# Graph attention and expert layers on one core: packets of one row for x and x1, and a longer lead for the gathers

## What is computed

```
def gnn(x):                                    # x is normalised row by row before this
    xt = matmul(x, weight).reshape(N, 4, 64)
    alpha = softmax(leaky_relu(einsum(xt[src], attn_l) + einsum(xt[dst], attn_r), 0.01), axis=1)
    tmp = einsum('nh,nhd->nd', alpha[:N], xt[dst[:N]])
    return broadcast(tmp, heads)               # the same 64 numbers for each head
x1  = x + gnn(layernorm(x))
z   = layernorm(x1)
out = x1 + z + sum over the 2 best of 8 experts e of  share_e * (gelu(z @ w1[e] + b1[e]) @ w2[e] + b2[e])
```

## Time and profile before

| | us |
|---|---|
| three runs: median (lowest to highest) | 481.96 (478.07 to 485.9) |
| the profiled execution: its own time | 482.41 |
| the profiled execution: span from the first to the last instruction | 480.7 |
| TensorE busy in the span | 385.5 |
| VectorE busy | 345.6 |
| ScalarE busy | 276.4 |
| GpSimd busy | 242.7 |

### The profile page before, as it was taken

How to read it: one execution, slowest core, us unless ns; L and a number is a source line. 1 busy time by engine, 2 the same in 40 slices (tenths; PEclk the granted TensorE clock), 3 DMA queues, 4 the chain that set the end, 5 groups by cost and what they waited for, 6 DMA issues and landing times.

```text
span 480.7 us, 11417 instructions
## 1 busy us (share of the span) xinstructions
PE 385.5 (80%) x3546; PEld 336.0 (70%) x3546; DVE 345.6 (72%) x1158; ACT 276.4 (58%) x715; POOL 242.7 (50%) x241
## 2 busy tenths in 40 slices
PE   3587999796999783545598989989999999999750
PEld 2476888685888673534487978878888788888740
DVE  1628859796979697969277868787788788778530
ACT  3138645363636364574176676777777777867530
POOL 7557867585848530000644544555644565554422
PEclk9597979596969796555599999999999999999885
DMA  4254725656565643021322322222222222221110
GB/s 149 76 150 135 198 78 152 194 154 197 152 191 140 203 121 124 14 92 55 81 62 75 82 64 65 68 80 81 74 65 68 84 88 68 81 69 58 58 44 20
DMA packets 18334, 48.23 MB, mean 100 GB/s; under 512 B 4719, under 2 KB 9354, under 8 KB 18276
## 3 DMA queue, kind: packets, MB, share of 16 engines
q0 software_dynamic: 10896, 29.61, 21.2%
q1 hardware_dynamic: 6626, 17.32, 12.1%
q10 hardware_dynamic: 756, 0.58, 0.4%
HBM read 34.42 MB, written 13.07 MB: 99 GB/s over the span
## 4 chain that ended last, share of the span: by engine, by line
PE 60%; DVE 13%; ACT 10%; issue 7%; DMA 4%; another core or an unknown queue 4%; POOL 1%; DVEq 0%; ACTq 0%; POOLq 0%
PE bank L1442 17%; PE bank L1425 16%; PE bank L1260 7%; PE bank L1389 4%; PE bank L1251 3%; PE bank L1284 3%; PE bank L1436 3%; PE bank L1263 3%; PE bank L1274 2%; DMA out_dram<-acc,order 2%; DMA work<-token_table,order 1%; PE bank L1375 1%; DVE row_out L986 1%; DVE work L955 1%
## 5 line engine op out<-in xcount | busy, mean ns | idle before, releaser
L475 POOL DMA_INDIRECT acc<-in_x_dram,index x98 | 112.5, 1148 | 53.7 <-ACT work L563 24.5
L512 POOL DMA_INDIRECT work<-token_table,order x76 | 74.8, 985 | 101.1 <-DVE order L1136 57.1
L693 ACT ACTIVATE h<-bank,b_col 128x128 f32<-128x128 f32 x250 | 78.0, 365 | 56.9 <-PE bank L1425 49.1
L1425 PE MATMUL bank<-work,w_hi 128*128 128x128 f16 x1000 | 100.0, 222 | 2.5 <-DVE work L1170 2.2
L1425 PE MATMUL bank<-work,w_lo 128*128 128x128 f16 x500 | 92.5, 222 | 0.0
L1425 PEld LDWEIGHTS bank<-work,w_hi 128*128 (+1 forms) x1000 | 83.2, 100 | 7.0 <-DVE work L1170 3.0
L521 POOL DMA_INDIRECT out_dram<-acc,order x49 | 49.5, 1011 | 75.7 <-DVE acc L1204 29.2
L1204 DVE SCALAR_TENSOR_TENSOR acc<-bank,work,acc 128x256 f32<-128x256 f32 (+1 forms) x125 | 60.4, 483 | 27.1 <-PE bank L1442 23.6
L1260 PE MATMUL bank<-w_ext,work 128*128 128x260 f32 x196 | 63.4, 454 | 16.3 <-ACT work L556 13.9
L1186 DVE SCALAR_TENSOR_TENSOR h_lo<-h,h_hi 128x256 f16<-128x256 f32 x125 | 52.6, 421 | 24.6 <-ACT h_hi L699 16.4
L1442 PE MATMUL bank<-w_hi,h_lo 128*128 (+1 forms) x250 | 69.2, 277 | 0.0
(11 more groups left out here) (208 smaller groups left out, 719.0 us busy)
## 6 DMA issues: line engine op xcount, KB each, us to landing
token_table<-row_out SPq DMA_DIRECT2D x7, 931.0 KB, 5.2
acc<-in_x_dram SPq DMA_DIRECT2D x7, 784.0 KB
work<-in_L_ffn_w_dram SPq DMA_DIRECT2D x16, 256.0 KB
acc<-in_x_dram,index POOLq DMA_INDIRECT x98
work<-token_table,order POOLq DMA_INDIRECT x76
out_dram<-acc,order POOLq DMA_INDIRECT x49
acc<-in_x_dram SPq DMA_DIRECT2D x7, 105.0 KB
w_raw<-in_L_gnn_weight_dram ACTq DMA_DIRECT2D x1, 256.0 KB
```

The source lines that it names most:

```text
L475: nc.gpsimd.indirect_dma_start(out=xds[:, t % RING, n, :], out_offset=None, in_=x, in_offset=bass.IndirectOffsetOnAxis(ap=index[:, n, t:t ...
L512: nc.gpsimd.indirect_dma_start(out=rows[:, k % ROWS_RING, :], out_offset=None, in_=table, in_offset=bass.IndirectOffsetOnAxis(ap=order[:, ...
L693: last = nc.scalar.activation(h32[:, i % RINGS, f * P:(f + 1) * P], bank[i % RINGS][:, f * P:(f + 1) * P], ACT.Gelu, bias=bias_of(f), scal ...
L1425: last = nc.tensor.matmul(bank[i % RINGS][:, f * P:(f + 1) * P], first_weights(i, lo, c, f), x2T[:, r, half, c * P:(c + 1) * P], start=(m ...
```

## The change

The padding of 16 numbers (APART) behind every row of `xres` and of `row_out` in SBUF keeps a partition's seven rows apart. The operations on them, the bytes moved and the layout in HBM stay. `x1T` moves up by 224 numbers a partition within `acc`. PACE goes from 5 to 8: tile t is gathered once tiles 0 to t - 9 are projected, and the wait begins with tile 9 instead of tile 6.

```
-PACE = 5
+PACE = 8
...
+APART = 16
...
-        xres = flat_acc[:, cut:cut + 2 * GT * D].rearrange("p (b t d) -> p b t d", b=2, t=GT)
-        cut += 2 * GT * D
+        xres = flat_acc[:, cut:cut + 2 * GT * (D + APART)].rearrange("p (b t d) -> p b t d", b=2, t=GT)[:, :, :, 0:D]
+        cut += 2 * GT * (D + APART)
         x1T = flat_acc[:, cut:cut + GT * D].rearrange("p (t k c) -> p t k c", t=GT, k=KT)
...
-        row_out = sb("row_out", [P, 2, GT, ROW])
+        row_apart = sb("row_out", [P, 2, GT, ROW + APART])
+        row_out = row_apart[:, :, :, 0:ROW]
```

## The result

| | before | after |
|---|---|---|
| median of 4 runs, side by side | 480.87 us (478.07 to 485.9) | 488.02 us (485.31 to 489.43) |
| profiled execution: span | 480.7 us | 487.1 us |

The ratio is 1.0218, with a 95% interval from 1.0173 to 1.0263. The prediction was 477.5 us.

What follows compares the result with a forecast made beforehand. No engine was full: each group loops through several, VectorE nearest its limit at some 84%. Terms 482.4 + 0 + 0 + 0 - 4.4 gave 478.0 us for a profiled execution, 477.5 for a median; range 467 to 488.

Steps and rivals of the forecast that it cites:

- (a): SP's loads of x: 1,024-byte packets instead of 7,168 are no slower, 2.6 to 3.2 us either way; term 0.
- (b): SP's x1 stores in 1,064-byte packets: last store delays expert pieces once, -1.0 to +2.1 us, taken as 0; 10.9 to 25.8 GB/s.
- The stall: ScalarE's wait for the last expert pieces, line 551: growth from 4.75 to 7 us would show slow small writes.
- (c): GpSimd's gathers start up to three tiles earlier; nobody waited for them, so direct gain 0.
- well under 17.6: Sign of being right: GpSimd's wait for ScalarE's copy at line 563 falls well under 17.6 us.
- (d): ScalarE's four "remote" idle stretches at group ends (4.23 to 7.10 us) shrink if long packets cause them; -4.4 us, a third of -13.1.
- the larger share for queue 0: Sign of being right: in windows with both queues loaded, queue 0 (the gathers) gets a larger share.
- The share of 0.8: Gathers' share beside x if DMA engines switch queues per packet: 0.8 with 1,024 against 4,096 bytes, 0.36 with 7,168.
- nothing happens: Rival: stretches belong to TensorE's completions under full DMA engines, however bytes are cut; 482 us, chance 0.30 (480 to 484).
- The slower one: Rival: extra gathers fall into store and expert pieces, 1.8 us more in each of four groups; 489 us, chance 0.12.
- Full relief: Rival: all four stretches go, with VectorE's 13.1 us; groups of 21.3 us, 468.9 us in all, chance 0.18.
- The four groups that I had counted: Seven-tile groups between 74.7 and 172.9 us, where VectorE's waits from the stretches total 13.1 us, the full-relief gain.

Runs made afterwards that it cites:

- eight at the start: Against the kernel before: lead of eight for the gathers of tiles 6 to 13 alone, five from tile 14, packets as before; 480.62 us, 1.0108.
- eight afterwards: Against the kernel before: lead of five for tiles 0 to 13, eight from tile 14 on, packets as before; 486.01 us, 1.0267.
- the run with eight and pauses: Against the kernel before: lead of eight, and at every third tile GpSimd waits until the gather of the tile before has landed; 508.67 us, 1.0507.
- the run with twelve gathers: Against the kernel before: lead of three for the first ten tiles, twelve extra gathers into unread memory behind tile 3's gather; 494.48 us, one execution.
- the last sitting: Fifth sitting: kernel before 456.82 us; x's padding alone, lead five, 455.3 us (0.9993); lead three for ten tiles plus delayed second x, 456.17 us (1.004).
- the run with narrow gathers: Lead of eight, gathers bringing 64 of each row's 256 numbers, the rest set to 1.0 by a VectorE memset; 495.72 us, one execution.

## Why the prediction was wrong

**(a) Packets of x, 0: right.** x was read at 0.84 MB in 4 us with a share of 0.770, 17.0 GB/s for one busy engine, against 17.9 in large pieces. SP's queue from 112 to 116 us in the kernel after:

```profile
q1 hardware_dynamic: 855, 0.84, 77.0%
```

**(b) Packets of x1, taken as 0, within -1.0 to +2.1: mis-sized.** The stall grew by 1.5 us (6.29 against 4.75), in the run with the padding alone by 2.2. The last store, at 192.9 to 197 us, alone on the queues:

```profile
q1 hardware_dynamic: 804, 0.86, 93.0%
```

That is 14.1 GB/s for one engine, nearer to the slow end of my range (10.9) than to the 18.2 and 25.8 of the large writes. I had taken reads of a row as the nearest row for writes of one. They were not. The 0.7 us that I had estimated beside the sum had the right sign and was too small.

**(c) The lead of eight, "Nobody waited for them, so the direct gain is 0": this is the step that failed.** The gain was indeed 0, but I stopped at it and never asked what GpSimd does to others while it issues. In the term's place the profiled executions show +6.6 us in the first group and +3.1 in the second, 9.7 together: increments of TensorE that reach ScalarE late while the lead fills. The lead of eight alone, without the padding, was slower by 1.8%; the runs with eight at the start and eight afterwards show that the cost stands where the lead fills, and the run with eight and pauses that it needs gathers issued back to back. It was not the only part of the loss (b adds 1.4), but the largest. From 40 to 180 us GpSimd is held 17.3 us by ScalarE, about as before (17.6 from 40 to 175): a lead that has filled is held by the same engine.

```profile
  ACT work L566: 17.3, 11
  issue: 17.2, 57
```

I had said "well under 17.6".

**(d) The stretches, -4.4: they gave nothing.** The third to sixth groups took 98.1 us, as before (98.2), and the stretches stayed. The reading of the earlier trace rows that the term rested on does not hold: its two windows stand 0.2 and 1.7 us behind the start of SP's issue of x (76.77 and 101.35 us), and it is this place that makes 0.017 and 0.344. Here is the gathers' queue at one place, 1 us behind that start, before (77.8 to 81.8 us) and after (87.5 to 91.5):

```profile
q0 software_dynamic: 45, 0.16, 23.9%
```
```profile
q0 software_dynamic: 43, 0.14, 15.6%
```

In the six loads with gathers beside them, each read in the 4 us from 1 us behind the start, it had 0.134 to 0.246 before and 0.010 to 0.191 after. So the larger share for queue 0 that I named as a sign did not come. In the first load after the change (40.4 to 44.4 us) the gathers moved one packet, though two had been issued at 41.17 and 42.42:

```profile
q1 hardware_dynamic: 993, 0.98, 97.9%
q0 software_dynamic: 1, 0.00, 1.0%
```

Packets of one row thus hold gathers back too, and the stretches don't come from long packets. The rival "nothing happens" was right on the stretches and missed the filling. The share of 0.8 that I had estimated from the turns in the Trainium skill ("DMA: Bandwidth & Descriptors", queues, rings and completion order) did not appear. Gathers alone fill a share of about 0.34 (the run with twelve gathers, 15 to 20 us), so most loads can't test the rule; the first load, with 0.010, speaks against it, since a gather was due there from about 42.8 us on (the first packets of the one issued at 37.44 came 1.6 us behind its issue).

**The rivals.** The slower one named 489 us, 1 us from the result, for the wrong reason: it put 1.8 us of load into each of four groups, and these four are no longer than before. The sign of it, that GpSimd goes on issuing with a lead of eight, is what happened, at the start. That the number is so near is luck. Full relief named groups of 21.3 us. They came in the last sitting, (175.8 - 36.8) / 6 = 23.2 us on average with 21.4, 20.7 and 21.1 in the third to fifth (x1 at 68.18, 89.59, 110.31 and 131.37), without the change. Its price was too small, though. The order of the tokens was there at 206.57 us instead of 229.25, 22.7 us earlier and not 13.1. The four groups that I had counted gave 14.0 of it; the rest lies in the first two groups (6.5) and behind the last x1 (2.2), where I had looked for nothing.

## What to carry to other kernels

That nobody waits for a transfer says that it may not be made earlier with profit; it does not say that making it earlier is free. Look at what the issuing engine does to the others while it runs ahead, and above all while the new lead fills, since that is paid even where the steady groups are unchanged. When an engine stands at another's semaphore and the profile calls it "remote", put the timelines of the other engines beside it, count the items on both sides (the profile may name the wrong one of several), find which of them begins and ends with the stretch, and test that engine's work by replacing it in place by other work. When two windows are compared, put them at the same place of the same event. And a difference between two sittings of the same kernel can be larger than any change under study, so compare only within one.

## What the runs showed of the hardware

- TensorE's increments reached ScalarE up to 11.0 us late while GpSimd issued indirect DMAs with pauses of 0.3 us (3.5 and 11.0 in the kernel after, 2.8 and 10.2 with twelve gathers put in); with iotas or plain DMAs from GpSimd in that place, or plain DMAs from the sync engine, the copies came within 0.1 us.
- VectorE was slowed as well: 27 memsets that wait for nothing took 3.6 us in the kernel after and 0.8 in the last sitting, and its wait for an increment of its own was 1.4 us there, 4.2 in the run with narrow gathers, and under 0.1 in the last sitting.
- The same kernel took 456.8 us in one sitting and 476 to 485 in four others, on the same chip as two of them. In both profiles of that sitting (of two kernels close to it) there was no such delay at all, with gathers issued for 47 us without a break in one.
- Beside a load of x in packets of 1,024 bytes the gathers' queue had a share of 0.010 to 0.191, with packets of 7,168 bytes 0.134 to 0.246.
- Plain DMAs cost GpSimd much less to issue than gathers: twelve took 6.51 us, 0.54 each, against 1.25 for a gather with its pause.
- Writes of 1,064 bytes ran at 14.1 GB/s for one busy engine, and reads of 1,024 bytes at 17.0.
- The time as a function of the lead has a sharp edge on one side (3: +8.0%, 4: +4.9%) and a flatter one on the other (6: +1.1%, not clear of noise; 8: +1.8%). This holds for the first four sittings; in the last no kernel with another lead throughout ran.
